# State-space layer of a hybrid kernel: the next batches' preparation put at other chunks, decay and inner products on pairs of row tiles

## The reference, cut to what matters

```python
x = x + conv_attention(group_norm(x))              # per batch, 1024 x 1024 scores
t = to_tokens(x)
t = t + _L1_attn_ref(_ln_t(t), ...)                # the state-space layer: the change is here
t = t + _L1_ffn_ref(_ln_t(t), ...)                 # 8 experts, top 2

def _L1_attn_ref(...):                             # 8 heads of 32, state of 32
    xn = _rmsnorm(x, norm_w)
    zxbcdt = einsum('bld,ed->ble', xn, W_in)       # gates z (256), x (256), B and C (64), dt (8)
    xBC = silu(causal_conv_of_4_taps(xBC) + conv_b)
    dt = softplus(dt + dt_bias); dA = exp(dt * -exp(A_log))
    # for each token: state = state * dA + (dt * x) outer B;  y = state . C
    y = y + Dp * xs
    y = _rmsnorm(y * silu(z), gnorm_w)
    return x + einsum('ble,de->bld', y, W_out)
```

## Time and profile before

| | |
|---|---|
| median of 3 runs | 1011.56 us |
| span of the profiled execution | 1012.5 us |
| TensorE, weight loads | 87%, 68% busy |
| VectorE | 73% busy |
| ScalarE, GpSimd | 52%, 25% busy |

### The profile page before, as it was taken

One profiled execution on the slowest core, in us unless ns is written; L12 is line 12 of the kernel. 1 busy time (PEld: TensorE's weight loads), 2 busy tenths in 40 slices (PEclk: granted clock), 3 DMA queues, 4 the chain that ended last, 5 costly groups with the idle time before them and its releaser, 6 DMA issues.

```text
span 1012.5 us, 19616 instructions
## 1 busy us (share of the span) xinstructions
PE 879.7 (87%) x7534; PEld 686.5 (68%) x7534; DVE 740.6 (73%) x1959; ACT 522.8 (52%) x796; POOL 250.1 (25%) x250
## 2 busy tenths in 40 slices
PE   3788999999988797979787979798779899989997
PEld 2556565656575675867566767676568788878887
DVE  2867677767766768696859595856968877878785
ACT  1525445544577465646464646453334665456543
POOL 0035111011100534343325252527520111011100
PEclk9879999999999697989799989899999999999999
DMA  5531000000003030302030303031000000000000
GB/s 146 177 134 22 11 11 21 22 11 12 21 1 67 7 73 5 70 20 54 10 64 2 73 2 73 2 73 64 2 1 1 22 22 22 1 22 22 22 3 40
DMA packets 30892, 36.13 MB, mean 36 GB/s; under 512 B 4560, under 2 KB 24912, under 8 KB 30800
## 3 DMA queue, kind: packets, MB, share of 16 engines
q1 hardware_dynamic: 29648, 30.68, 12.4%
q10 hardware_dynamic: 1152, 4.19, 1.1%
HBM read 21.50 MB, written 4.98 MB: 26 GB/s over the span
## 4 chain that ended last, share of the span: by engine, by line
PE 60%; DVE 25%; ACT 6%; issue 5%; POOL 2%; SPq 0%; DMA 0%; DVEq 0%; ACTq 0%; POOLq 0%
PE ps L1028 7%; PE ps L699 6%; DVE cacc L1693 4%; PE ps L950 4%; PE ps L686 4%; PE ps L778 3%; DVE acc L1970 3%; PE ps L780 3%; PE ps L779 3%; PE ps L653 3%; PE ps L941 2%; PE ps L658 2%; ACT un L1359 2%; PE ps L934 2%; PE ps L675 2%
## 5 line engine op out<-in xcount | busy, mean ns | idle before, releaser
L1970 DVE SCALAR_TENSOR_TENSOR acc<-ps,comb,acc 128x128 f32<-128x128 f32 x512 | 141.2, 344 | 22.2 <-PE ps L1028 21.7
L1028 PEld LDWEIGHTS ps<-w_f,hid 128*128 128x128 f32 x1024 | 131.2, 191 | 16.2 <-ACT hid L1378 8.0
L1378 ACT ACTIVATE hid<-ps,b_f 128x512 f32<-128x512 f32 x128 | 86.1, 685 | 107.5 <-PE ps L780 107.4
L1028 PE MATMUL ps<-w_f,hid 128*128 128x128 f32 x1024 | 136.8, 276 | 4.6 <-ACT hid L1378 4.6
L569 POOL TENSOR_TENSOR srs<-sve,neg_half 128x1 f32<-128x1 f32 x64 | 50.8, 794 | 217.3 <-DVE gram L1802 217.3
L1550 DVE TENSOR_REDUCE nmax<-ps 128x1 f32<-128x1024 f32 x64 | 78.1, 1221 | 30.7 <-PE ps L658 30.4
L1693 DVE SCALAR_TENSOR_TENSOR cacc<-ps,cw,cacc 128x1023 f32<-128x1023 f32 (+5 forms) x72 | 91.8, 1275 | 10.4 <-ACT cacc L1250 9.6
L1319 ACT ACTIVATE dcy<-ps 128x1024 f32<-128x1024 f32 x64 | 65.0, 1016 | 59.0 <-PE ps L901 58.9
L1166 ACT ACTIVATE probs<-ps,nmax 128x1024 f32<-128x1024 f32 x64 | 71.2, 1113 | 38.7 <-DVE nmax L1550 35.8
L1785 DVE SCALAR_TENSOR_TENSOR dcy<-dcy,g_sb 128x1024 f32<-128x1024 f32 x64 | 86.1, 1346 | 0.1
L686 PEld LDWEIGHTS ps<-id_f,probs 128*128 128x128 f32 x512 | 59.9, 144 | 33.1 <-issue 23.5
(11 more groups left out here) (212 smaller groups left out, 1905.0 us busy)
## 6 DMA issues: line engine op xcount, KB each, us to landing
c_dec<-exp_dram SPq DMA_DIRECT2D x32, 256.0 KB, 5.2
xc<-in_x SPq DMA_DIRECT2D x8, 512.0 KB, 3.6
q_b<-q_a SPq DMA_DIRECT2D x16, 256.0 KB, 2.8
X<-in_x_tok ACTq DMA_DIRECT2D x8, 512.0 KB, 5.5
c_rep<-cacc SPq DMA_DIRECT2D x32, 128.0 KB, 3.1
out<-o_ch SPq DMA_DIRECT2D x8, 512.0 KB, 2.6
w_f<-in_w SPq DMA_DIRECT2D x2, 512.0 KB, 4.2
cst_f<-in_sel_rows SPq DMA_DIRECT2D x1, 512.0 KB, 4.5
```

Of the source, the lines that this page charges most:

```text
L1028: last = nc.tensor.matmul(ps[:, Y_BANKS[n], t * P:(t + 1) * P], hid[n % 2][:, t * P:(t + 1) * P], w2_f[:, e, :], start=True, stop=True)
L1378: nc.scalar.activation(hid[n % 2][:], ps[:, 4 + n % 2, :], ACT.Gelu, bias=b1_f[:, n // 2:n // 2 + 1]).then_inc(e_hidden_ready, 1)
L1970: done = nc.vector.scalar_tensor_tensor(acc[u][:, tt, :], ps[:, bank, t * P:(t + 1) * P], comb[u][:, tt, e:e + 1], acc[u][:, tt, :], ALU.m ...
```

## The change

- `decay` runs as two products on two row tiles of 64 rows each (rows 0 to 63 into bank 4, rows 64 to 127 into bank 5) instead of two with all 128 rows. The mask for tokens that come later is coded for quads of tokens (32 rows) instead of pairs (64 rows), so that each half holds all it needs. `rhs_c` is half as long; SyncE reads 8 transfers a batch instead of 4.
- `inner_products` takes its eight products alternately from rows 0 and rows 64, into the two banks. For that the convolution and SiLU of group 2 run on 128 partitions instead of 64; the weights already held B and C twice.
- The parts get other slots on all four engines, in another order in places; `normed` runs three batches ahead.

```diff
-        rhs_c = [sb(f"rhs_c{u}", [P, NH, P], F32R) for u in range(2)]
+        rhs_c = [sb(f"rhs_c{u}", [P, NH // 2, P], F32R) for u in range(2)]
...
-                for part in range(2):
-                    rows = cum_dram[u, part].rearrange("(c h) t -> c h t", h=NH)
-                    sp.dma_start(rhs_c[u][NT * part:NT * part + NT].bitcast(F32), rows).then_inc(m_rows_read, 16)
-                    rows = cum_dram[u, part].rearrange("(c h) t -> h c t", h=NH)
-                    r0 = 2 * NT + NH * part
-                    sp.dma_start(lhs_c[u][r0:r0 + NH].bitcast(F32), rows).then_inc(m_rows_read, 16)
+                for half in range(2):
+                    for part in range(2):
+                        rows = cum_dram[u, part].rearrange("(c k h) t -> k c h t", k=2, h=NH // 2)[half]
+                        r0 = 2 * DS * half + NT * part
+                        sp.dma_start(rhs_c[u][r0:r0 + NT].bitcast(F32), rows).then_inc(m_rows_read, 16)
+                        rows = cum_dram[u, part].rearrange("(c h) t -> h c t", h=NH)
+                        r0 = 2 * DS * half + 2 * NT + NH * part
+                        sp.dma_start(lhs_c[u][r0:r0 + NH].bitcast(F32), rows).then_inc(m_rows_read, 16)
...
-            pool_parts = [(totals, (), 3.5), (decayed, (0,), 3.5), (decayed, (1,), 4.5), (weighted, (0,), 5.5),
-                          (weighted, (1,), 6.5)]
+            pool_parts = [(weighted, (0,), 1.5), (totals, (), 2.5), (decayed, (0,), 2.5), (decayed, (1,), 3.5), (weighted, (1,), 6.5)]
...
-                for t in range(NT):
+                for k in range(NT):
+                    t, r0 = k // 2 + NT // 2 * (k % 2), 2 * DS * (k % 2)
                     r = slice(t * P, (t + 1) * P)
-                    last = nc.tensor.matmul(cols(hi_banks, t, P), cacc[b % 3][0:DS, 2, r], c_rep[0:DS, r],
-                                            start=True, stop=True)
+                    last = nc.tensor.matmul(cols(hi_banks, t, P), cacc[b % 3][r0:r0 + DS, 2, r], c_rep[r0:r0 + DS, r],
+                                            start=True, stop=True, tile_position=(r0, 0))
...
                 for h in range(2):
-                    done = nc.tensor.matmul(ps[:, 4 + h, :], lhs_c[u][:, c, :],
-                                            rhs_c[u][:, 4 * h:4 * h + 4, :].rearrange("p h t -> p (h t)"),
-                                            start=True, stop=True)
+                    rows = slice(2 * DS * h, 2 * DS * (h + 1))
+                    done = nc.tensor.matmul(ps[:, 4 + h, :], lhs_c[u][rows, c, :],
+                                            rhs_c[u][rows].rearrange("p h t -> p (h t)"),
+                                            start=True, stop=True, tile_position=(2 * DS * h, 0))
...
-            pe_parts = [(gates, (0, 0), 1, 0), (gates, (0, 1), 1, 0), (gates, (1, 0), 1, 0.5), (gates, (1, 1), 1, 0.5), (turn_x, (0,), 1, 2), (turn_x, (1,), 1, 2), (turn_normed, (), 2, 2.5),
-                        (inner_products, (), 1, 2.5), (steps, (), 2, 3.5), (turn_b, (), 1, 3.5),
-                        (group, (0, 0), 2, 3.5), (group, (0, 1), 2, 3.5), (group, (1, 0), 2, 4.5),
-                        (group, (1, 1), 2, 4.5), (group, (2, 0), 2, 5.5), (group, (2, 1), 2, 5.5), (cumulate, (), 2, 7)]
+            pe_parts = [(gates, (0, 0), 1, 0), (gates, (0, 1), 1, 0), (gates, (1, 0), 1, 1), (gates, (1, 1), 1, 1), (turn_x, (0,), 1, 1.5), (turn_x, (1,), 1, 1.5), (turn_normed, (), 2, 2), (inner_products, (), 1, 2), (steps, (), 2, 2.5), (group, (0, 0), 2, 2.5), (group, (0, 1), 2, 2.5), (turn_b, (), 1, 3.5), (group, (1, 0), 2, 4), (group, (1, 1), 2, 4), (group, (2, 0), 2, 4.5), (group, (2, 1), 2, 4.5), (cumulate, (), 2, 6.5)]
...
-                nc.scalar.activation(cacc[b % 3][0:2 * DS, 2, :], cacc[b % 3][0:2 * DS, 2, :], ACT.Silu).then_inc(m_silu_ready, 1)
+                nc.scalar.activation(cacc[b % 3][:, 2, :], cacc[b % 3][:, 2, :], ACT.Silu).then_inc(m_silu_ready, 1)
...
+                    if first and c == 0:
+                        normed(2, 0)
...
-            act_parts = [(silus, (), 1, 0.5), (normed, (), 2, 1.5), (gather_x, (), 1, 2),
-                         (high, (), 2, 2.5), (steps, (), 2, 3.5), (gather_b, (), 1, 3.5), (tap, (0,), 2, 3.5),
-                         (tap, (1,), 2, 4.5), (softplus, (), 2, 4.5), (tap, (2,), 2, 5.5), (shortcut, (), 1, 6.5),
-                         (factors, (), 2, 7.5)]
+            act_parts = [(silus, (), 1, 0.5), (gather_x, (), 1, 1.5), (high, (), 2, 2), (steps, (), 2, 2.5), (tap, (0,), 2, 2.5), (softplus, (), 2, 3), (gather_b, (), 1, 3.5), (shortcut, (), 1, 3.5), (tap, (1,), 2, 4), (normed, (), 3, 6), (tap, (2,), 2, 6), (factors, (), 2, 7)]
...
-                    rows = P if g < 2 else 2 * DS
+                    rows = P
...
-            dve_parts = [("conv", (2, 3), 1, -0.25), ("ends", (), 1, 1), ("low", (), 2, 2.75), ("inner", (), 1, 3),
-                         ("steps", (), 2, 4), ("conv", (0, 1), 2, 4), ("conv", (0, 2), 2, 4.5),
-                         ("conv", (0, 3), 2, 4.75), ("softplus", (0,), 2, 5), ("conv", (1, 1), 2, 5.5),
-                         ("softplus", (1,), 2, 5.75), ("conv", (1, 2), 2, 6), ("conv", (1, 3), 2, 6.5),
-                         ("exponents", (), 2, 7), ("conv", (2, 1), 2, 7), ("conv", (2, 2), 2, 7.5)]
+            dve_parts = [("conv", (2, 2), 1, 0), ("conv", (2, 3), 1, 0), ("ends", (), 1, 1), ("low", (), 2, 2), ("inner", (), 1, 2), ("steps", (), 2, 2.75), ("conv", (0, 1), 2, 2.75), ("conv", (0, 2), 2, 3), ("softplus", (0,), 2, 3.5), ("conv", (0, 3), 2, 4), ("softplus", (1,), 2, 4), ("conv", (1, 1), 2, 4.5), ("conv", (1, 2), 2, 5), ("conv", (1, 3), 2, 5.5), ("exponents", (), 2, 6.75), ("conv", (2, 1), 2, 7)]
```

More of the change, by code:

```diff
@@ L423, in spread @@
                     sp.dma_start(cst_f[:, 0, :], sel_rows).then_inc(mamba_weights_loaded, 16)
-                    sp.dma_start(cst_f[:, 1, :], head_rows).then_inc(mamba_weights_loaded, 16)
+                    sp.dma_start(cst_f[:, 1, 0:BANK], head_rows).then_inc(mamba_weights_loaded, 16)
             load_pictures(0, 4)
@@ L473, in decay_rows @@
                     spread_c(b)
-                sp.wait_ge(m_rows_read, 64 * (b + 1))
+                sp.wait_ge(m_rows_read, 128 * (b + 1))
                 sp.sem_inc(wait_carrier, 1)
@@ L894, in decay @@
                 if c == 0:
-                    pe.wait_ge(m_rows_read, 64 * (b + 1))
+                    pe.wait_ge(m_rows_read, 128 * (b + 1))
                 if n == 0:
@@ L1497, in decay_operands @@
                 dst = (lhs_c, rhs_c)[side][u]
-                nc.vector.tensor_copy(dst[:].rearrange("p c t -> p (c t)"), cst_f[:, side, :])
+                n = dst.shape[1] * P
+                nc.vector.tensor_copy(dst[:].rearrange("p c t -> p (c t)"), cst_f[:, side, 0:n])
             def low_weights():
@@ L1730, in exponents @@
                     if not isinstance(b, int) or b > 0:
-                        dve.wait_ge(m_rows_read, 64 * b)
+                        dve.wait_ge(m_rows_read, 128 * b)
                     sums = sum_banks(b)
@@ L2053 @@
     full = np.ones((32, 8, 128), np.float32)
-    pair = np.arange(64)[:, None]
-    pair_of = np.tile(np.arange(128) // 2, 8)[None, :]
-    none = np.zeros((32, 1024), np.float32)
+    quad = np.arange(32)[:, None]
+    quad_of = np.tile(np.arange(128) // 4, 8)[None, :]
+    head_of = (head * full).astype(np.float32).reshape(32, 2, 512)
+    after = np.where(quad_of < quad, np.float32(-1e30), np.float32(0.0))[:, 0:512]
     b2_blocks = np.zeros((8, 8, 8, 128), np.float32)
@@ L2073 @@
         "ones": np.ones((128, 128), np.float32),
-        "sel_rows": np.concatenate([(sel * full).astype(np.float32).reshape(32, 1024), none,
-                                    (pair_of == pair).astype(np.float32)]),
-        "head_rows": np.concatenate([(head * full).astype(np.float32).reshape(32, 1024), none,
-                                     np.where(pair_of < pair, np.float32(-1e30), np.float32(0.0))]),
+        "sel_rows": np.tile(np.concatenate([(sel * full).astype(np.float32).reshape(32, 1024),
+                                            (quad_of == quad).astype(np.float32)]), (2, 1)),
+        "head_rows": np.concatenate([head_of[:, 0], after, head_of[:, 1], after]),
         "router": g["L1_ffn_router_w"].T,
```

## The result

The changed kernel takes 1005.59 us in the median of 5 runs (1000.18 to 1007.83), the kernel before 1011.73 beside it (1008.58 to 1013.18): ratio 0.9932, interval 0.9907 to 0.9958. It is 6 us faster, where 24.5 were forecast. The profiled execution has a span of 1003.6 us against 1012.5.

The account below looks back on a forecast made before the run. TensorE bounds chunks 0 to 4, VectorE 5 to 7, with a stall at `cumulate` between. Scan 0 and tail -4.5, scans 1 to 5 -17.3, scan 6 -1.0, before scan 0 -1.7: 1012.5 becomes 988.0, median 987, range 974 to 1005.

Parts of the forecast that it names:

- the price of 0 for the copy of C: Inner products at c2: `c_rep` lands 3.1 us after issue in the median, 1.7 us before it is wanted; cost 0.
- A regular scan: Scan 4, slots followed chunk by chunk between gatings: 50.5 us by reckoning before, 47.0 after.
- What is late next: TensorE's `group(2)` waits about 3 us for the third `conv(0)` at c4; VectorE sets the end, so counted once.
- Rival (a): Stall moves to `group(2)` or inner products (`c_rep`), TensorE falls to 1.2 GHz: 49.5 us a scan, 999 us; chance 0.18.
- Each us later is a us for each scan: Copy of C before the inner products at c2: past its narrow cover, every us of lateness lengthens each scan by one.
- Scan 0 and its tail, -4.5: Second gating of scan 0 to first of scan 1: loses the pile at 7.5, 47.8 us become 43.3.
- The stops for no semaphore: TensorE stops such as 3.35 us in scan 3, part of why scans 1 to 5 average 53.1 us; left unchanged.
- The stretch before scan 0, -1.7: Inner products ahead of scan 0 run at 1.2 GHz on the path: a gain of 1.7 us.
- The lock: VectorE instructions all in SBUF wait for running GpSimd ones: `decayed(1)` beside `softplus(0)` +1.7 us, L1720 loses 1.1, L1708's stays.
- Tile pairs: Pairs of 64-row tiles overlap fully: inner products go from 1.97 to about 1.0 us; the decay gains nothing.
- Rival (c): Tile pairs sharing their columns do not overlap, inner products stay at 1.97 us: 994 us; chance 0.05.
- Rival (d): 3 us idle at c4.5 leaves TensorE at 1.2 GHz through c5 to c7, +8 us a scan: 1027 us; chance 0.07.

Follow-up runs that it names:

- e_order: Changed kernel with SyncE issuing the copy of C ahead of `c_dec` instead of behind it: 991.3 us, ratio 0.9797 to the kernel before.
- e_decay_whole: Changed kernel with `decay` on whole rows again, mask for pairs, four row reads instead of eight: 997.23 us, ratio 0.9865 to the kernel before.
- e_both_decay_whole: Changed kernel, copy of C ahead of `c_dec`, GpSimd's `totals` and `decayed` two slots later, `decay` on whole rows: 970.9 us, ratio 0.9600 to before.

## Why the prediction was wrong in size, point by point

The step that failed is the price of 0 for the copy of C, the second point. With only that put right (`e_order`) the kernel takes 991.3 us, within the forecast's 980 to 994.

- **A regular scan: right, with one term mis-sized.** 47.8 us against 47.0. Chunks 0 to 7 came out at 4.99, 4.49, 7.19, 8.96, 7.24, 6.53, 3.13 and 5.26; forecast were 4.9, 4.5, 7.3, 8.7, 7.8, 4.9, 3.6 and 5.3. The one that failed is c5; that the total is off by only 0.8 is partly luck, since c4 and c6 came out 0.6 and 0.5 short. The text gives c1 as 4.5 with loads of 3.4 / 5.8 and does not say why its length is not the larger; in the trace the increments, 1.2 us of that load, run before the gating of c0. "What is late next" was named rightly, `group(2)` behind the third `conv(0)`, and at the right size (3 us forecast, 3.8 measured). But it was counted as covered by VectorE. It is not: behind it TensorE is at the low clock (L953 then takes 1.99 us at 596.45, granted clock 0.52, one of the text's own signs of being wrong), and c5 takes 1.6 us more, as the projections and L953 come late and at that clock. Rival (a) was this mechanism, and named the wait for `c_rep` too, at a price of 2.5 us a scan.
- **The copy of C: the step that failed.** The text said "Price 0 with a narrow cover", from a landing of 3.1 us in the median. Two things were wrong. The median of single issues is not the time of the copy: the inner products need the last of four pieces, issued 1.9 us after the first. And the cover was worked out with a median over all scans, while in scans 0 and 1 of the kernel before each piece had already taken 5.4 to 6.1 us. In scans 0 and 1 the copy's issue stands behind `c_dec`, and it landed 7.6 and 7.9 us after its first issue, so TensorE stood 3.59 and 2.69 us, then ran cold. The bound row was there, 6.1 us for the longest landing. `e_order` prices the step: 5.6 and 4.3 us in scans 0 and 1, 12.5 between the first gating and the last with the shorter stop of scan 3, 14.3 in the medians.
- **"Each us later is a us for each scan": half right.** In scans 0 and 1 it was worse than one for one, through the clock. In scan 4 the last piece landed at 572.73 and the products began at 573.47, so 0.7 us of cover were left, and scans 2 to 6 show no wait for it.
- **Scan 0 and its tail, -4.5: wrong in sign, through the copy.** The text takes it from the second gating of scan 0 to the first of scan 1: 47.8 us before, 49.5 in the changed kernel, 44.1 in `e_order` against the 43.3 forecast. So with the copy on time this term was nearly right. What stays short is the rest of scan 1, where `e_order` gains 0.8 us and the forecast has 2.9 (0.8 of 3.6): c5 takes 6.47 there instead of 4.9, and the stall at `cumulate` was smaller in that scan before (c7 took 7.49 us, not 8.69), so less could be gained.
- **The stops for no semaphore, "I leave those as they are": not so.** The one in scan 3 went from 3.35 to 5.04 us, and over the kernels of this study it lay between nothing and 5.35. A cost of this size that no program line sets is a part of the range, not a constant.
- **The stretch before scan 0, -1.7: right for the products, not seen in the time.** The inner products ahead of scan 0 take 1.66 us instead of 3.78, but begin at 331.49 us instead of 329.63, and the first gating stands at 350.4 us against 349.9. The attention ahead of it, the same work in both kernels, had other stretches at the low clock (mean granted clock 0.99 instead of 0.86 in the first 50 us, 0.94 instead of 1.00 from 250 to 300). In the other kernels the first gating lies between 346.8 and 353.5, so a gain of 1.7 us there can't be read from one profile.
- **The lock: right where it was predicted, wrong in its weight.** L1718 takes 1.98 us (forecast: up to 2), L1720 fell from 1.36 to 0.21, and one small instruction for dt still takes 2.1 us (L1705, where L1708 was forecast, as the slots differ by an instruction). The Trainium skill (SBUF — State Buffer, "SBUF: two separate sides") describes an exclusive lock: of a VectorE instruction with two SBUF inputs and a GpSimd instruction that reads SBUF, the later one waits for the whole of the other. The traces agree: 2.09 us beside GpSimd's 2.10 and 0.22 without it. The prediction booked the collisions as VectorE time that stays, and did not ask what stands behind them: taken away, they give 2.9 us in a regular scan and shorten the wait of `group(2)` there to 1.6 us or less.
- **Tile pairs: right.** Sixteen records of L889 take 1.16 us with their pipeline's end, L887 took 2.05; the forecast was about 1.0 from 1.97, and the pairs start together. Rival (c), that they do not overlap, is out. The decay pair gains nothing, as forecast: both records start together, but L953 behind it takes 1.13 instead of 1.02 us. Its four reads more, "0.3 us each", were put beside other work; `e_decay_whole` shows them on the path: in its profile scans 0 and 1 are 2.2 and 4.3 us shorter, with 0.7 and 1.6 us less of the wait. The tiles of the decay go back with the reads there, so it prices both together.
- **Rival (d), slower: did not come.** TensorE is cold behind the 3.8 us at `group(2)`, but recovers within the chunk.

Together: the span came out 15.6 us above the 988.0 forecast. With the copy on time (`e_order`, span 991.9) 3.9 us are left, of which 3.1 lie before the first gating (351.3 us instead of 348.2). From the first gating to the last `e_order` takes 368.7 us, 22.3 less than the kernel before (391.0), where the forecast has 22.8. That the two totals agree so closely is partly luck, since the parts erred in both directions: too much for scan 1, too little for scans 2 and 6 (5.1 and 2.3 us shorter against 3.6 and 1.0).

## What to carry to other kernels

Price a transfer by the last piece that the reader needs, from the issue of the first, in the place where its queue is fullest, and not by the median of its issues; where the cover is as narrow as here (1.7 us reckoned, 0.7 left in scan 4), look at what is queued ahead of it, and try the order first. TensorE's waits for C of 2.7 and 3.6 us, and of 5.2 at `cumulate` before, were paid twice in these kernels, once as idle time and once as products at the low clock behind them. When parts are moved, look which GpSimd instruction now runs beside small VectorE instructions between SBUF tiles: moving the GpSimd work by two slots gave 2.9 us in a regular scan and 14.6 us in all, where the whole change gave 6.

## What the runs showed that was not expected

**A packet of code beside the stop in scan 3.** TensorE stops inside the increments of scan 3 (L918, in the kernel before L915), after 106 of 112 records, for no semaphore. In each kernel with such a stop one packet of 0.02 MB on the queue named "instruction" falls shortly before TensorE goes on. DMA queues of the changed kernel from 513 to 514 us (packets, MB, share of 16 engines); TensorE goes on at 516.12:

```profile
q1 hardware_dynamic: 356, 0.17, 117.0%
q8 instruction: 1, 0.02, 9.0%
```

The same packet in `e_both_decay_whole`, the kernel without the stop, between 484 and 485 us; its increments begin at 488.46:

```profile
q1 hardware_dynamic: 88, 0.04, 15.3%
q8 instruction: 1, 0.02, 7.2%
```

In nine kernels that stop, with stops of 1.94 to 5.35 us, the packet stands 2.3 to 2.9 us ahead of the instruction that goes on; in the one without, 3.7 us ahead of the whole group and some 4.8 ahead of its 107th record. So the stop ends a near-constant time after the packet, and is longer the later the packet comes. That TensorE waits for this packet is argued from these distances alone. What makes it late is open: the changed kernel has `c_dec` and the copy of C on the other queue at that moment, but `e_order` has a stop of 2.27 us with its packet at 501 to 502 us, where the other queue moved nothing. A kernel that moves only the traffic around that moment was not tried.
